# Last layer of a four-stage block: int8-to-bf16 copies first in each ScalarE slot, and an end written out by hand

## The reference

```python
def _L1_ffn_ref(x, w1, conv_w, conv_b, w2):      # D_MODEL 512, D_HIDDEN 2048
    def act_quant(x):
        scale = 127.0 / jnp.clip(jnp.max(jnp.abs(x), axis=-1, keepdims=True), 1e-05)
        return jnp.clip(jnp.round(x * scale), -128, 127) / scale
    ...
    h = bit_linear(x, w1)                        # act_quant(x) by ternary weights
    h = depthwise_conv1d(h.transpose(0, 2, 1), conv_w, conv_b)   # 3 taps along the tokens
    h = jax.nn.silu(h.transpose(0, 2, 1))
    return bit_linear(h, w2)                     # act_quant(h): one maximum per token over 2048 channels
x = x + jnp.tanh(g_ffn[1]) * _L1_ffn_ref(x, L1_ffn_w1, L1_ffn_conv_w, L1_ffn_conv_b, L1_ffn_w2)
```

## Time and profile before

| | us |
|---|---|
| median of 3 runs | 1800.57 (1794.78 to 1801.24) |
| the profiled execution, whole | 1798.3 |
| its span, first to last instruction | 1796.5 |
| the slots of the last layer, up to the last `add_out` | about 1416 to 1792 of the span |
| DVE busy, whole span | 1276.3 (71%) |
| PE busy, whole span | 1556.9 (87%) |
| ACT busy, whole span | 883.3 (49%) |

### The profile page before, as it was taken

One profiled execution on the slowest core, in us unless ns is written; L12 is line 12 of the kernel. 1 busy time (PEld: TensorE's weight loads), 2 busy tenths in 40 slices (PEclk: granted clock), 3 DMA queues, 4 the chain that ended last, 5 costly groups with the idle time before them and its releaser, 6 DMA issues. The chain is left out here.

```text
span 1796.5 us, 25689 instructions
## 1 busy us (share of the span) xinstructions
PE 1556.9 (87%) x9559; PEld 948.6 (53%) x9559; DVE 1276.3 (71%) x2065; ACT 883.3 (49%) x1430; POOL 574.0 (32%) x556
## 2 busy tenths in 40 slices
PE   6798888987678889878999998999996878888886
PEld 4444444443355658645666665666664534444443
DVE  5576778888443546744777776767766699999995
ACT  4455555555444336435334343343332577777763
POOL 3132343233210012123112111220200497777770
PEclk9899999999788889989999999999999899999999
DMA  5112221222723434521020110201011411111111
GB/s 167 41 48 95 94 72 47 72 71 94 281 77 96 165 103 141 192 101 48 1 83 24 59 60 25 72 34 59 13 47 36 180 62 65 65 65 65 53 48 47
DMA packets 73284, 142.34 MB, mean 79 GB/s; under 512 B 8418, under 2 KB 17782, under 8 KB 72907
## 3 DMA queue, kind: packets, MB, share of 16 engines
q1 hardware_dynamic: 71914, 137.55, 22.2%
q0 software_dynamic: 960, 3.15, 0.6%
q10 hardware_dynamic: 288, 0.00, 0.0%
HBM read 97.67 MB, written 43.01 MB: 78 GB/s over the span
## 5 line engine op out<-in xcount | busy, mean ns | idle before, releaser
L2859 POOL TENSOR_TENSOR E_y<-E_y,E_centre 128x1024 f32<-128x1024 f32 x64 | 151.6, 2369 | 10.4 <-ACT E_y L2888 8.2
L2774 PE MATMUL E_OP<-E_w2q,E_yb 128*128 128x512 bf16 x512 | 128.3, 408 | 25.2 <-issue 18.9
L1454 ACT ACTIVATE D_oT<-D_OB 128x512 fp32r<-128x512 f32 x64 | 38.3, 598 | 219.5 <-DVE D_OB L1771 219.5
L2851 POOL TENSOR_SCALAR E_centre<-E_hs,E_cw,E_cb 128x512 f32<-128x512 f32 x64 | 106.9, 1670 | 59.7 <-DVE E_hs L2941 59.4
L2764 PE MATMUL E_HP<-E_xT,E_w1q 128*128 128x512 bf16 x512 | 123.3, 385 | 0.4 <-ACT E_xT L2865 0.2
L1743 DVE TENSOR_TENSOR D_q_low<-D_PJ,D_q_high 128x512 fp32r<-128x512 f32 x60 | 41.5, 691 | 98.7 <-ACT D_q_high L1430 98.7
L2950 DVE SCALAR_TENSOR_TENSOR E_y<-E_hs,E_cw,E_y 128x512 f32<-128x512 f32 x128 | 104.5, 855 | 1.1 <-POOL E_y L2859 1.1
L2774 PEld LDWEIGHTS E_OP<-E_w2q,E_yb 128*128 128x128 bf16 x512 | 52.1, 104 | 94.5 <-issue 47.2
L1523 PE MATMUL D_PJ<-D_xT_high,D_wq_high 128*128 128x512 f32 x240 | 101.7, 424 | 0.1
L588 PE MATMUL A_TX<-A_wo,A_oT 128*128 128x512 f32 x176 | 90.9, 642 | 7.1 <-PEq L1106 7.1
L1523 PE MATMUL D_PJ<-D_xT_high,D_wq_low 128*128 128x512 f32 x240 | 94.9, 395 | 0.0
(11 more groups left out here) (427 smaller groups left out, 4130.0 us busy)
## 6 DMA issues: line engine op xcount, KB each, us to landing
A_res<-in_x SPq DMA_DIRECT2D x8, 1024.0 KB, 5.3
xn_d<-A_xn SPq DMA_DIRECT2D x8, 1024.0 KB, 4.7
x_d<-A_res SPq DMA_DIRECT2D x8, 1024.0 KB, 5.9
W_raw<-in_w1T SPq DMA_DIRECT2D x16, 512.0 KB, 3.6
W_raw<-in_w2T SPq DMA_DIRECT2D x16, 512.0 KB, 3.9
D_res<-x_d SPq DMA_DIRECT2D x8, 1024.0 KB, 6.1
x_d<-D_res SPq DMA_DIRECT2D x8, 1024.0 KB, 4.4
E_res<-x_d SPq DMA_DIRECT2D x8, 1024.0 KB, 5.4
```

The costliest lines, as they stand in the source:

```text
L2774: mm = pe.matmul(OP[:, :], yb[:, k, c * P:(c + 1) * P], w2q[:, k, :], start=k == 0, stop=k == MC - 1)
L2851: pool.tensor_scalar(U[i % 2][:, 0, :], hs[i % NBUF][:, 0, 1:TILE + 1], cw[:, 2 * p, 1:2], cb[:, 2 * p:2 * p + 1], ALU.mult, ALU.add).then ...
L2859: pool.tensor_tensor(y, y, U[i % 2][:, :, :], ALU.add).then_inc(t0, 1)
```

## The change

Three things, all in `ternary_layer`. In ACT's loop, `to_bf16` moves from the end of its slot to its start, ahead of `products`, and `unit_out` moves from behind `silu` to just behind `products`. The loops stop after tile 7 and what follows is written out by hand, in another order. In that end the maxima of pairs 61 and 63 are taken from HP's first half (`turn_bank`), so that transposes alternate between two pairs of banks; the last tile's four chunks each have a bank of HP (`out_bank`), so that `project_out` no longer waits for the `add_out` before it; and chunk 0 of the last tile is quantised and copied in two parts of 8 channel rows.

```diff
+        LAST, END = STEPS - 1, MP * STEPS
+        def parts(n, c):
+            return 2 if (n, c) == (LAST, 0) else 1
+        def out_bank(n, c):
+            return HP[:, 1 - c // 2, c % 2, :] if n == LAST else OP[:, :]
+        def turn_bank(i):
+            return HP[:, 0, :, :].rearrange("p b (c e x) -> p (b c) e x", e=2, x=P) if i in (END - 3, END - 1) else YT[:, :, :, :]
...
             def project_out(n, c):
-                pe.wait_ge(qb, SUB * n + c + 1)
-                need(pe, o_ok, SUB * n + c)
-                for k in range(MC):
-                    mm = pe.matmul(OP[:, :], yb[:, k, c * P:(c + 1) * P], w2q[:, k, :], start=k == 0, stop=k == MC - 1)
+                if n < LAST:
+                    need(pe, o_ok, SUB * n + c)
+                for part in range(parts(n, c)):
+                    pe.wait_ge(qb, pieces_done(n, c, part))
+                    tiles = channel_tiles(n, c, part)
+                    for k in range(tiles.start, tiles.stop):
+                        mm = pe.matmul(out_bank(n, c), yb[:, k, c * P:(c + 1) * P], w2q[:, k, :],
+                                       start=k == 0, stop=k == MC - 1)
                 mm.then_inc(o_mm, 1)
...
             def turn_y(i):
                 pe.wait_ge(sil, i + 1)
-                need(pe, amk, i)
+                need(pe, amk, i if i < END - 3 else i - 1)
+                if i == END - 3:
+                    pe.wait_ge(h_s, END - 1)
...
-            for n in range(STEPS + 2):
+            for n in range(STEPS):
                 for p in range(MP):
                     i = MP * n + p
-                    if n < STEPS:
-                        products(n, p)
+                    if p in CAST:
+                        s = n - 1 if p else n - 2
+                        if 0 <= s:
+                            to_bf16(s, CAST.index(p))
+                    products(n, p)
+                    if p == CAST[0] and 1 <= n:
+                        unit_out(n - 1)
                     if n + 1 < STEPS and p < 2:
                         keep_xT(n + 1, p)
-                    if 0 <= i - LAG < MP * STEPS:
+                    if 0 <= i - LAG:
                         silu(i - LAG)
-                    if p in CAST:
-                        if p == CAST[0] and 1 <= n <= STEPS:
-                            unit_out(n - 1)
-                        s = n - 1 if p else n - 2
-                        if 0 <= s < STEPS:
-                            to_bf16(s, CAST.index(p))
+            silu(END - 2)
+            to_bf16(LAST - 1, 3)
+            silu(END - 1)
+            unit_out(LAST)
+            for c in range(SUB):
+                for part in range(parts(LAST, c)):
+                    to_bf16(LAST, c, part)
```

More of the change, by code:

```diff
@@ L2667, in ternary_layer, with channel_tiles, pieces_done @@
         QUANT, CAST, OUT, ADD = (4, 5, 6, 7), (5, 6, 7, 0), (7, 1, 3, 5), (6, 0, 2, 4)
+        LAST, END = STEPS - 1, MP * STEPS
+        def parts(n, c):
+            return 2 if (n, c) == (LAST, 0) else 1
+        def channel_tiles(n, c, part):
+            size = MC // parts(n, c)
+            return slice(part * size, (part + 1) * size)
+        def pieces_done(n, c, part):
+            return SUB * n + c + part + 1 + (n == LAST and c > 0)
+        def out_bank(n, c):
+            return HP[:, 1 - c // 2, c % 2, :] if n == LAST else OP[:, :]
+        def turn_bank(i):
+            return HP[:, 0, :, :].rearrange("p b (c e x) -> p (b c) e x", e=2, x=P) if i in (END - 3, END - 1) else YT[:, :, :, :]
         r_dr, out_dr = tile_view(io["x3_d"]), tile_view(io["out"])
@@ L2814, in _ @@
                         pe.wait_ge(last.added, SUB)
-                    if n < STEPS:
-                        project_in(n, p)
+                    project_in(n, p)
                     if i == 1:
@@ L2823, in _ @@
                         turn(n + 1, p - 1)
-                    if 1 <= n <= STEPS and p == FOLD + 1:
+                    if 1 <= n and p == FOLD + 1:
                         spread(n - 1)
@@ L2827, in _ @@
                         done = n - 1 if p == MP - 1 else n - 2
-                        if 0 <= done < STEPS:
+                        if 0 <= done:
                             project_out(done, OUT.index(p))
+            turn_y(END - 5)
+            turn_y(END - 4)
+            project_out(LAST - 1, 1)
+            turn_y(END - 3)
+            turn_y(END - 2)
+            turn_y(END - 1)
+            project_out(LAST - 1, 2)
+            spread(LAST)
+            project_out(LAST - 1, 3)
+            for c in range(SUB):
+                project_out(LAST, c)
         @block.gpsimd
@@ L2865, in keep_xT, with to_bf16 @@
                 act.activation(XT[n % 2][:, 2 * half:2 * half + 2, :], TX[:, :, :], ACT.Copy).then_inc(x_te, 1)
-            def to_bf16(n, c):
-                act.wait_ge(q8, SUB * n + c + 1)
+            def to_bf16(n, c, part=0):
+                act.wait_ge(q8, pieces_done(n, c, part))
                 need(act, o_mm, SUB * (n - 1) + c + 1)
-                toks = slice(c * P, (c + 1) * P)
-                act.activation(yb[:, :, toks], y8[:, :, toks], ACT.Copy).then_inc(qb, 1)
+                toks, tiles = slice(c * P, (c + 1) * P), channel_tiles(n, c, part)
+                act.activation(yb[:, tiles, toks], y8[:, tiles, toks], ACT.Copy).then_inc(qb, 1)
             def products(n, p):
@@ L2971, in units, with quantise @@
                 dve.reciprocal(ru[:, :], un[:, :]).then_inc(ru_ok, 1)
-            def quantise(n, c):
+            def quantise(n, c, part=0):
                 dve.wait_ge(sp_mm, n + 1)
                 need(dve, qb, SUB * (n - 1) + c + 1)
[L2976 to L2979, removed]
+                toks, tiles = slice(c * P, (c + 1) * P), channel_tiles(n, c, part)
+                dve.tensor_tensor(y8[:, tiles, toks], Y[n % 2][:, tiles, toks],
+                                  SBK[:, toks].rearrange("p (a t) -> p a t", a=1)
+                                  .to_broadcast([P, tiles.stop - tiles.start, P]), ALU.mult).then_inc(q8, 1)
             def add_out(n, c):
@@ L2984, in add_out @@
                 dve.wait_ge(f_ok, n + 1)
-                dve.scalar_tensor_tensor(out=R[n % 2][:, c, :], in0=OP[:, :], scalar=f2[n % 2][:, c:c + 1],
+                dve.scalar_tensor_tensor(out=R[n % 2][:, c, :], in0=out_bank(n, c), scalar=f2[n % 2][:, c:c + 1],
                                          in1=R[n % 2][:, c, :], op0=ALU.mult, op1=ALU.add).then_inc(o_ok, 1)
@@ L3008, in _ @@
                               .to_broadcast([P, MC, 2 * STEPS]), ALU.mult).then_inc(hh_ok, 1)
-            for n in range(STEPS + 2):
+            for n in range(STEPS):
                 for p in range(MP):
                     i = MP * n + p
-                    if 0 <= i - FOLD < MP * STEPS:
+                    if 0 <= i - FOLD:
                         biggest(i - FOLD)
-                    if n < STEPS and i > 0:
+                    if i > 0:
                         scale(n, p)
-                    if 0 <= i - LAG < MP * STEPS:
+                    if 0 <= i - LAG:
                         right_taps(i - LAG)
-                    if 1 <= n <= STEPS:
+                    if 1 <= n:
                         if p == FOLD - 1:
@@ L3024, in _ @@
                         done = n - 1 if p == ADD[0] else n - 2
-                        if 0 <= done < STEPS:
+                        if 0 <= done:
                             add_out(done, ADD.index(p))
+            right_taps(END - 2)
+            biggest(END - 4)
+            right_taps(END - 1)
+            add_out(LAST - 1, 1)
+            for i in range(END - 3, END):
+                biggest(i)
+            units(LAST)
+            add_out(LAST - 1, 2)
+            for part in range(parts(LAST, 0)):
+                quantise(LAST, 0, part)
+            quantise(LAST, 1)
+            add_out(LAST - 1, 3)
+            quantise(LAST, 2)
+            add_out(LAST, 0)
+            quantise(LAST, 3)
+            for c in range(1, SUB):
+                add_out(LAST, c)
 _OUT_SHAPE = (NB, S, D)
```

7 lines of the change are left out of this document (4 added, 3 removed).

## The result

The changed kernel took 1784.54 us (median of 4 runs, 1781.27 to 1786.13), the kernel before beside it 1800.02 (4 runs, 1794.78 to 1801.24): ratio 0.9917, 95% interval 0.9893 to 0.9942. The forecast was 1785.5 in 1780 to 1792.5. Timed again later, with six runs beside 11 of before, the same program had a median of 1789.49 beside 1800.20, ratio 0.9932 (0.9906 to 0.9957).

What follows compares the result with a forecast made beforehand. The prediction took DVE to bound the loop, waiting only for the output projection (10.1 us). Savings of 5.9 + 1.4 + 7.05 = 14.35 us took 1798.3 to 1783.9, adjusted toward the median to 1785.5, range 1780 to 1792.5.

Steps and rivals of the forecast that it cites:

- the sum of 14.35: All predicted savings together: 5.9 in the loop, 1.4 in slot 2 and 7.05 at the end, in us.
- Copy first: In ACT's loop, earlier bf16 copies remove DVE's waits before chunk 0: 7.05 us off, 5.9 of it in tiles 1 to 6.
- The wait goes at either clock: Chunk 0's projection, started early, ends before DVE asks at 1570.6, whether it takes 3.62 or 5.13 us.
- Slot 2: Taps slowed inside POOL's add end sooner: 0.2 us in five tiles, 0.4 in tile 7, 1.4 in all; bounds 0 and 4.3.
- The chunk-1 wait stays: DVE's five loop waits before chunk 1, 0.61 us each, remain because no copy is in their chain.
- rival A: TensorE's idle time and low clock move to chunk 1's projection, costing up to 1.7 us in five tiles: 1792.3, chance 0.09.
- C: The end gives less because projection (6, 2) and half the next run at low clock: 11.2 us off, 1788.7, chance 0.12.
- The end: After the last tile-6 quantise, reordering and separate banks bring the last add from 1791.46 to 1784.4; 5.85 us excluding add_out(6, 0)'s 1.2.
- Rival B: Waits before chunk 0 were often absent, leaving only the end and slot 2: 7.3 us off, about 1787 to 1793, chance 0.13.
- Rival D: Late copies push POOL's adds into DVE's taps, 1.24 us more per pair: slower, 1803 to 1838, chance 0.04.

Runs made afterwards that it cites:

- e12: The changed kernel, unedited, timed and profiled again: median 1789.49 us, ratio 0.9932 to the kernel before.
- e3: The kernel before with 12 overwritten filler matmuls in TensorE's idle time ahead of chunk 0's projection, copy still late: ratio 0.9960 to the kernel before.
- e11: The changed kernel with projection (6, 2) in an HP bank between the transposes of 61 and 62, plus 16 filler matmuls before those of 60: ratio 0.9915.
- e10: The kernel before with 4 and 8 filler matmuls ahead of the transposes of 61 and 62 in its old end: last layer 372.6 us, single run.
- e1: The kernel before with only ACT's copies moved first in the slots of tiles 1 to 7, old end kept: ratio 0.9935 to the kernel before.
- e4: The changed kernel with the last tile's four chunks in one bank, each projection waiting for the add before: ratio 0.9947 to the kernel before.
- e7: The changed kernel with 4 and 8 filler matmuls behind the transposes of 61 and 62: ratio 0.9925 to the kernel before.
- e8: The changed kernel with projection (6, 2) in a bank of HP, between the transposes of 61 and 62: ratio 0.9927 to the kernel before.
- e5: The changed kernel with all transposes in one bank pair (YT), each group waiting for the maxima before: last layer 366.1 us, single run.
- e6: The changed kernel with chunk 0 of the last tile in one piece instead of halves: last layer 359.6 us, single run.
- e9: The e7 kernel, filler in the end, with all transposes in one bank pair (YT): last layer 362.0 us, single run.
- e2: The changed kernel with ACT's loop in the old order, copies behind products and silu, new end kept: ratio 0.9973 to the kernel before.

## Why the prediction was right

The direction and the time were right. So was the mechanism of both parts: an early copy lets the projection follow `project_in` at once, and the end is freed of its waits for the bank. But that the sum of 14.35 met the 14.4 between the two profiled executions is luck: errors cancelled. In the last layer the profiled execution gained 12.4 (375.4 to 363.0); another 1.9 are a last layer that began sooner (1414.1 against 1416.0), with no edit before it. The second profile (e12) gained 13.8 there.

- *Copy first, 7.05 us forecast, 8.8 measured.* The sum counted the idle time before each add. The pitch of two tiles shows what such a wait costs, 1.26 us (44.40 to 43.14): the add starts 1.04 late (ready at 1570.59), and the maxima come 0.88 and not 0.66 after it, since nothing overlapped. Seven times 1.26 is 8.8, as L fell in e3.
- *Why it helps.* "The wait goes at either clock" was hardly put to the test: with the copy first the projection of chunk 0 took 3.62 us in every tile of every profile but one (4.05 in e11, without a wait). e3 and tile 2 of e10 show that a late copy costs nothing at the high clock. What the move does is to take away PE's idle time ahead of the projection.
- *Slot 2, 1.4 us forecast, 0.4 measured.* The taps do fall from 2.64 to 2.23. But e3, with 2.64, has the same pitch. With the shorter taps the add of chunk 2 is ready sooner and then waits for PE (projection until 1542.71, add at 1542.75 in the changed kernel), and the maxima come 0.87 after it, not 0.66: from taps to maxima it is 3.24 us, against 3.23 in e3. Only tile 7, without input transposes, gains: pitch 41.80 in e1, 42.22 in e3. In the other tiles the lower bound of 0 was the right value.
- *The chunk-1 wait stays:* five, near 0.6, as said. In the changed kernel and in e1, e4, e7, e8 and e12 one of five grew by 0.8 to 1.0; in e5 one grew by 0.8 and a sixth of 1.17 came; in e6, e9 and e11 none did. That is rival A, at one tile per execution and not five: its price was 8.4 and is mostly about 0.9. In the other tiles the low clock covers transposes and `project_in` and costs nothing. (The prediction's 1792.3 for A starts from the profiled execution; on the footing of 1785.5, as for C, it is 1793.9.)
- *The end, 5.85 us forecast, 4.0 measured* (5.1 in e12). Of the 5.85 about 5.6 lie in M+F. F was to be 17.1 and is 17.65: the projection of (6, 3) waits for the add of (6, 2), a step I had left out (0.45; e8 takes it away). M was to be 15.8 (1751.49 to 1767.3) and is 16.85. The low clock took the transposes of 63 too (1.94 us, 0.85 more), and the projection took 5.53 in place of 5.30. In e12, with 1.06 and 5.30 as forecast, M is 15.78. The single banks hold 4.8 us of F (e4) and the halves 0.7 (e6), though F fell by 4.5 in all; order and bank pair together are worth 0.6 at the full clock (e10 against e7), and the order without the pair would be about 2 slower than the old one (e9 against e10).
- *Rival B* fell in part: every profile of the old loop without filler had the waits, but not in each tile (six of seven in e2, five in e10). *Rival D* fell: copies ahead of products delay none, and outside slot 2 the one pair of taps that begins in POOL's add is the one that was worked out (2.29 us at 1744.87).

## What to carry to other kernels

Read a wait with the clock of what it waits for: here a late copy looked like the cause, but its harm was that TensorE idled 3.15 us and then ran at 1.2 GHz; filler matmuls in the gap gave the loop the same gain (8.8 us, against 8.7 for the copy first), though 1.6 of it was lost again in the end. A wait costs more than its idle time where the next instruction would have overlapped, so take it from the pitch of two like stretches, one with it and one without. And an idle time that is moved takes its low clock along: look at what now stands behind it, and whether the waiting engine has room there.

## What was not expected of the hardware

The old loop's drop came at the same place in all seven tiles of the first profile and cost 1.26 us in the pitch of a tile; behind the same 3.15 us of idle time it stayed out once in e10. In the end of the layer the same instructions up to that point had their 16-matmul projection at 3.62, 5.30 and 5.53 us in three executions (e6, e12, changed), and M at 14.10, 15.78 and 16.85, so one profile of such a stretch is good to no better than about 2.8 us. Filler did not always remove the drop: in three of the five profiles with filler (e3, e10, e11), and in none of the nine without, the projection of (6, 3) was slow, 5.09, 5.30 and 5.81 us (F 23.71, 23.84 and 19.41). The Trainium skill, "SBUF — State Buffer", section "SBUF: two separate sides", has the port pair shared between GpSimd and VectorE as an exclusive lock. By that rule POOL's centre tap must wait too when DVE's taps hold the pair, and the trace of before agrees: 0.76 us at 1416.81, beside no taps, and in the loop 1.70 to 1.78 us beside them, as at 1541.50:

```profile
1416.81 0.76 POOL L2851 TENSOR_SCALAR E_centre<-E_hs,E_cw,E_cb 128x512 f32<-128x512 f32 x1
...
1541.31 1.41 DVE L2950 SCALAR_TENSOR_TENSOR E_y<-E_hs,E_cw,E_y 128x512 f32<-128x512 f32 x2
1541.50 1.70 POOL L2851 TENSOR_SCALAR E_centre<-E_hs,E_cw,E_cb 128x512 f32<-128x512 f32 x1 [0.75 <-DVE E_hs L2941]
```
